# Four graph layers on one core: the first two mask units of layers 0 and 1 are made during the dense product, and the last group of layer 3 is multiplied tile by tile

## What is computed

```python
# layer 0 (4 heads of 64; layer 1 is the same form with slope 0.2 and no elu)
h = einsum('nf,hfd->hnd', x, W)
s_src = einsum('hnd,hd->hn', h, a[:, :64, 0]); s_dst = einsum('hnd,hd->hn', h, a[:, 64:, 0])
e = leaky_relu(s_src[:, :, None] + s_dst[:, None, :], 0.01)
alpha = softmax(where(adj == 0, -inf, e), axis=-1)
out = elu(einsum('hij,hjd->hid', alpha, h))
# layer 2: one wide head with a gated side branch (matrix work only, unchanged here)
# layer 3
t = tanh(x @ W + b); e = (t @ a)[:, 0]; valid = sum(t, axis=1) != 0
w = where((adj > 0) & valid, exp(e - max), 0)
out = (w / sum(w)) @ (x @ W)
```

## Time and profile before

| | us |
|---|---|
| median of 3 runs | 3078.27 |
| lowest and highest of them | 3075.31, 3078.79 |
| the profiled execution, by the same clock | 3075.53 |
| its span in the trace | 3073.7 |
| PE busy in it | 2958.1 (96%) |
| DVE, ACT, POOL busy | 2141.2, 1921.2, 1171.3 |
| mean granted clock of PE | 0.989 |

### The profile page before, as it was taken

One profiled execution on the slowest core, in us unless ns is written; L12 is line 12 of the kernel. 1 busy time (PEld: TensorE's weight loads), 2 busy tenths in 40 slices (PEclk: granted clock), 3 DMA queues, 4 the chain that ended last, 5 costly groups with the idle time before them and its releaser, 6 DMA issues.

```text
span 3073.7 us, 65208 instructions
## 1 busy us (share of the span) xinstructions
PE 2958.1 (96%) x24628; PEld 2584.4 (84%) x24628; DVE 2141.2 (70%) x3861; ACT 1921.2 (63%) x3414; POOL 1171.3 (38%) x1555
## 2 busy tenths in 40 slices
PE   7899999999979999999999999999999999889998
PEld 6799999999969999999997877887778778655554
DVE  4998888888879888888886556665666565562245
ACT  4777898999979999999995544454455444430000
POOL 0571375642225656564221023333323332534222
PEclk9999999999999999999999999999999999989999
DMA  8566200000100000000010000000000000000001
GB/s 285 184 215 234 70 14 11 14 11 15 60 12 12 14 11 14 11 14 11 14 34 12 4 1 4 4 1 4 1 4 4 1 1 1 2 1 0 1 21 35
DMA packets 41977, 104.55 MB, mean 34 GB/s; under 512 B 9921, under 2 KB 23489, under 8 KB 33601
## 3 DMA queue, kind: packets, MB, share of 16 engines
q1 hardware_dynamic: 39584, 101.61, 10.0%
q10 hardware_dynamic: 2208, 0.52, 0.1%
HBM read 97.73 MB, written 4.39 MB: 33 GB/s over the span
## 4 chain that ended last, share of the span: by engine, by line
PE 77%; DVE 2%; ACT 2%; issue 1%; POOL 1%; POOLq 0%; DVEq 0%; ACTq 0%
PE bank L1318 16%; PE bank L1315 16%; PE bank L1372 15%; PE bank L1410 12%; PE bank L1321 11%; PE bank L1399 2%; PE bank L1256 2%; PE bank L1386 1%; ACT above L932 0%; PE bank L1527 0%; DVE rings L1931 0%; ACT rings L1072 0%; DVE rings L1936 0%; ACT values L845 0%; PE bank L1494 0%
## 5 line engine op out<-in xcount | busy, mean ns | idle before, releaser
L1315 PE MATMUL bank<-values,rings 128*128 128x195 bf16 x8192 | 1415.9, 247 | 43.4 <-DVE rings L1936 39.7
L1318 PE MATMUL bank<-values,rings 128*128 128x195 bf16 x8192 | 1416.1, 249 | 0.0
L932 ACT ACTIVATE above<-srow,kpass 128x512 fp8e4<-128x512 f32 x2048 | 1290.2, 709 | 124.2 <-DVE rings L1936 118.0
L1315 PEld LDWEIGHTS bank<-values,rings 128*128 128x128 fp8e4 x8192 | 806.9, 98 | 53.2 <-issue 51.0
L1318 PEld LDWEIGHTS bank<-values,rings 128*128 128x128 fp8e4 x8192 | 789.5, 96 | 0.7
L1931 DVE TENSOR_TENSOR rings<-rings,above 128x512 uint32<-128x512 uint32 x512 | 399.2, 780 | 186.5 <-PE bank L1318 165.4
L1025 ACT ACTIVATE values<-srow,cmul 128x512 f32<-128x512 f32 x256 | 205.8, 814 | 428.0 <-PE bank L1410 427.2
L1936 DVE TENSOR_TENSOR rings<-rings 128x512 uint32<-128x512 uint32 x512 | 431.2, 842 | 17.2
L1410 PE MATMUL bank<-hv,values 128*128 128x257 f32 x1792 | 420.6, 380 | 0.0
L1410 PEld LDWEIGHTS bank<-hv,values 128*128 128x128 f32 x1792 | 335.0, 190 | 69.9 <-issue 25.2
L1321 PE MATMUL bank<-values,rings 128*128 128x390 bf16 x2032 | 338.6, 329 | 13.4 <-DVE values L1730 13.4
(11 more groups left out here) (217 smaller groups left out, 3445.0 us busy)
## 6 DMA issues: line engine op xcount, KB each, us to landing
arena<-in_adj_dram SPq DMA_DIRECT2D x64, 1024.0 KB, 5.1
srow<-src_dram SPq DMA_DIRECT2D x69, 256.0 KB, 3.1
x<-in_x_dram SPq DMA_DIRECT2D x4, 1024.0 KB, 12.5
out_dram<-x SPq DMA_DIRECT2D x7, 512.0 KB, 2.9
arena<-in_L_gnn_fe_w_dram SPq DMA_DIRECT2D x2, 512.0 KB, 6.2
arena<-in_L_gnn_W_hz_dram SPq DMA_DIRECT2D x1, 1024.0 KB, 7.3
arena<-in_L_gnn_g_w_dram SPq DMA_DIRECT2D x1, 1024.0 KB, 10.8
weights<-in_L_gnn_W_dram SPq DMA_DIRECT2D x3, 256.0 KB, 3.8
```

The source lines that it names most:

```text
L932: last = act.activation(above[:, k % 2, q, :], srow[:, par, :], ACT.Relu, scale=BIG, bias=kpass[:, p % 2, k * Q + q:k * Q + q + 1], satura ...
L1315: pe.matmul(acc[:, 0:KW], pos[:, k % 2, q, :].bitcast(FP8)[:, rows], v[:, 0:KW], start=start, stop=final, skip_group_check=True)
L1318: last = pe.matmul(acc[:, KW:2 * KW], neg[:, k % 2, q, :].bitcast(FP8)[:, rows], v[:, KW:2 * KW], start=False, stop=final, skip_group_chec ...
```

## The change

1. **Masks ahead.** In layers 0 and 1 PE spreads the first row after quad 3 (`first_row`, into bank 7) instead of after the last quad. ACT copies it in quad 4 and writes two of the eight `above` pieces of units 0 and 1 in each of the quads 4 to 7 (`above_ahead`), from column scores of the first eight tiles that DVE scales early (`first_keys`). DVE makes the masks of both units before `stats` (`masks_ahead`). At the start of attention the values of round 0 stand alone.
2. **Row factors later.** POOL's `row_factors` waits for the first two values, and ACT takes their exponential at the end of its group 0.
3. **Weights of layer 0.** The loads of `a` are two transfers instead of eight, and `fold_first_weights` does four instructions twice as wide instead of eight.
4. **Layer 2 to 3.** POOL adds the bias of the pairs 10 to 13. In layer 3's unit 1, `first_lasts` of round 0 goes ahead of `first_products` of round 1.
5. **Last group.** During group 6 DVE makes a second copy of masks, those of group 7 (eight instructions, into the arena). PE then does group 7 one bank after the other, 32 matmuls each (`last_tiles`). DVE takes out group 6 and normalises the quads 5 and 6 after group 6's units, and normalises each tile of the last quad at once; SP stores each by itself.

The diff, cut to its core:

```diff
+UNITS_AHEAD = 2
+ROW_AT, KEYS_AT = 3, 2
+BY_POOL = range(10, 14)
...
-            for t in range(T - QT, T, 2):
-                sp.wait_ge(s_xmade, T * NORMS[4] + t + 2)
-                sp.dma_start(out[t * P:(t + 2) * P, :].rearrange("(t p) f -> p t f", p=P), x[:, t:t + 2, :])\
-                    .then_inc(s_out, 16)
+            for t in range(T - QT, T):
+                sp.wait_ge(s_xmade, T * NORMS[4] + t + 1)
+                sp.dma_start(out[t * P:(t + 1) * P, :], x[:, t, :]).then_inc(s_out, 16)
...
+        edge_last = arena[:, 0:BITS * Q * WORDS].bitcast(U32).rearrange("p (k q w) -> p k q w", k=BITS, q=Q)
...
             def row_factors(l):
-                pool.wait_ge(s_shift, l + 1)
+                pool.wait_ge(s_vfirst, first_values_before(l) + 2)
...
+                for n in BY_POOL:
+                    pool.wait_ge(E.l_h, n + 1)
+                    pool.wait_ge(E.l_score, n - 1)
+                    pool.tensor_tensor(low3[n % 2], h[:, n * ET:(n + 1) * ET, :],
+                                       bvec[:, :].unsqueeze(1).to_broadcast([P, ET, F]), ALU.add).then_inc(E.l_inpool, 1)
...
+            def copy_row(l):
+                act.wait_ge(s_rowps, l + 1)
+                act.activation(srow[:, 0, :], bank[7][:, :], ACT.Copy).then_inc(s_srow[0], 16)
+
+            def above_ahead(l, n):
+                k, q = divmod(2 * n, Q)
+                if n == 0:
+                    act.wait_ge(s_kfirst, l + 1)
+                    act.wait_ge(s_srow[0], (l * H * NG // 2 + 1) * 16)
+                if q == 0:
+                    act.wait_ge(s_sides, l * H * UNITS + k - 1 + CREDIT)
+                for q in (q, q + 1):
+                    last = act.activation(above[:, k % 2, q, :], srow[:, 0, :], ACT.Relu, scale=BIG,
+                                          bias=kpass[:, 0, k * Q + q:k * Q + q + 1], saturate=False)
+                if q == Q - 1:
+                    last.then_inc(s_above, 1)
...
-                for hd in range(H):
-                    act.dma_start(avec[:, s, hd * D:(hd + 1) * D],
-                                  A["L0_gnn_a"][hd, s * D:(s + 1) * D, 0].partition_broadcast(P)).then_inc(s_w, 16)
+                act.dma_start(avec[:, s, :].rearrange("p (h d) -> p h d", h=H),
+                              A["L0_gnn_a"][:, s * D:(s + 1) * D, 0].partition_broadcast(P)).then_inc(s_w, 16)
...
                         copy_quad_xT(l, q)
+                        if l < 2 and q == ROW_AT + 1:
+                            copy_row(l)
+                        if l < 2 and q > ROW_AT:
+                            above_ahead(l, q - ROW_AT - 1)
                         copy_quad_h(l, q)
...
+            def first_row(l):
+                pe.wait_ge(s_h, T * l + GT + 1)
+                if l == 0:
+                    pe.wait_ge(s_packed, ROW_AT - 1 + CREDIT)
+                for it in range(GT):
+                    last = pe.transpose(bank[7][:, it * P:(it + 1) * P],
+                                        scores[:, 0, it:it + 1].to_broadcast([P, P]), ident[:, :])
+                last.then_inc(s_rowps, 1)
...
+            def last_tiles(slot, par):
+                for it in range(GT):
+                    rows = slice(it * P, (it + 1) * P)
+                    for j in range(T):
+                        if it == 0 and j % Q == 0:
+                            pe.wait_ge(s_lastedge, j // Q + 1)
+                        last = pe.matmul(bank[GT * par + it][:, 0:2 * KW],
+                                         edge_last[:, j // Q, j % Q, :].bitcast(FP8)[:, rows], values[:, slot, j, :],
+                                         start=(j == 0), stop=(j == T - 1))
+                    last.then_inc(s_bank, 1)
...
+            def masks_ahead(l):
+                chain.enter(0, LINKS[l])
+                if l == 0:
+                    dve.wait_ge(s_packed, GT + CREDIT)
+                for k in range(UNITS_AHEAD):
+                    for _ in masks(l, TURN[l] * H * UNITS + k, k, packed[:, :, 0:WORDS]):
+                        pass
...
-                      1: ((first_products, 1), (first_lasts, 0), (first_rests, 1), (first_products, 2), (first_lasts, 1)),
+                      1: ((first_lasts, 0), (first_products, 1), (first_rests, 1), (first_products, 2), (first_lasts, 1)),
...
-                with dve.Fori(1, NG // 2) as gg:
+                with dve.Fori(1, NG // 2 - 1) as gg:
                     for par in range(2):
                         group(3, gg * 2 + (last_pass + par), gg, par, 1 - par, norm=gg * 2 + (par - 2))
+                group(3, last_pass + NG - 2, NG // 2 - 1, 0, 1, norm=NG - 4, last_edges=True)
+                evacuate(3, 0, 0, last_pass + NG - 1)
+                chain.enter(NG - 3, 2)
+                for k in (2, 3, 4, 6, 7):
+                    output_norm(QUADS - 3, k)
                 chain.leave(NG - 2)
-                for k in (2, 3, 4):
+                for k in (2, 3, 4, 6, 7):
                     output_norm(QUADS - 2, k)
                 last_rows()
```

147 lines of the change are left out of this document (86 added, 61 removed).

## The result

The changed kernel takes 3058.54 us in the median of four runs (3057.64 to 3061.66), the kernel before 3077.03 in the runs beside them: a ratio of 0.9946, 95% interval 0.9935 to 0.9958. Faster by 0.54%, or 18.5 us by these medians. Three later groups of runs of the kernel before had medians of 3076.41, 3076.13 and 3076.16, and four more runs of the changed kernel had 3059.67, so the gain is 16.5 to 18.5 us. The prediction was 3060.5, range 3054 to 3067.

What follows compares the result with a forecast made beforehand. PE was taken as the bound, busy 2958.1 of 3073.7 us. Terms 1.4 - 0.5 + 5.7 + 5.5 + 0.9 + 1.3 + 2.3 = 16.6 us gave 3058.9 (profiled base) or 3061.7 (median); predicted 3060.5, range 3054 to 3067.

Steps and rivals of the forecast that it cites:

- Start of layer 0: Wait for folded weights before PE's first product: two loads 0.3 us and wide fold 1.1 us, 1.4 earlier; bounds 0.5 and 4.
- rival of a still earlier start: Layer 0: both loads of a land with the first of eight, dense product up to 5 us earlier; total 3057.5, chance 0.08.
- The row in the dense product: Layers 0 and 1: four spreading transposes move between quads, where PE is waited for, costing 0.5 us in each layer.
- Layer 0, first group: Start of layer 0's attention: PE starts 4.2 us earlier, later units 5.8; term 5.7, bounds 4.2 and 6.5.
- given back later: Layer 0, groups 1 to 3: DVE sets the pace, both first groups' 11.2 us are lost; total 3070.1, chance 0.10.
- Layer 1, first group: Start of layer 1's attention: unit 2 begins 6.0 us earlier, less 0.5 for the row; term 5.5, bounds 3.6 and 7.
- Between layers 2 and 3: Four bias adds moved from DVE to POOL: 3.8 us per two pairs against 4.2, gain 0.9; bounds -0.5 and 2.4.
- POOL and DVE slow each other: Lower bound for moving four bias adds to POOL between layers 2 and 3: -0.5 us instead of a gain.
- fear of the program change: Reduction before layer 3 follows POOL's last add and needs a change of POOL's program: may take 0.4 us, at most 1.
- Start of layer 3: Last parts of round 0 move ahead of round 1's products: gain 1.3 us, bounds 0.5 and 1.5.
- The end: PE's end to DVE's last normalisation: 8.2 us instead of 10.5, gain 2.3; bounds 0 and 5.
- Masks late: Layers 0 and 1: unit 1's `above` delays DVE's masks, `stats` slips up to 3.6 us each; total 3067.5, chance 0.05.

## Why the prediction was right, and where it was not

The sum was 16.6 us and the gain is 16.5 to 18.5. The mechanism came true in its largest part, the masks ahead, and the total also by luck, as the terms show:

- **Start of layer 0**: 1.4 predicted, 2.5 to 2.8 measured. The fold's 1.1 was right. The step that failed is "Two loads carry the same bytes, so I take 0.3 us for them": it was 1.45. The bound of 4 held it. The rival of a still earlier start had the mechanism but asked for 5. In the kernel without masks ahead only 1.65 of the 2.5 reach the end of group 0, and 1.35 the pass near 498, so the 1.4 is near what the start is worth by luck.
- **The row in the dense product**: 0.5 predicted, 0.43 measured in layer 1, from its first dense product to the statistics (40.71 before, 41.14 in all eight profiles with the row). In layer 0 the clock's differences, of up to 1 us there, hide it.
- **Layer 0, first group**: PE's start 4.2 earlier against the statistics, predicted and measured (10.70 to 6.48). The further 1.5, from DVE's shorter list, came in whole in four profiles (39.44 against 40.91) and by 0.4 or less in the other four (40.76), with the place of the clock's lower stretches. At group 0 the sum has 1.4 - 0.5 + 5.7 = 6.6; the eight profiles have 5.9 to 8.4. Of this lead 0.15 to 0.65 us went again by group 8 in six of them, one gained 0.6, and one lost 2.6, 1.5 of it at a lower stretch near 267. With what the early start loses, "given back later" has that much truth.
- **Layer 1, first group**: 5.5 predicted, 4.8 to 5.4 measured.
- **Between layers 2 and 3**: +0.9 predicted, -0.15 to -0.6 measured. The step that failed is the sum "Tanh 0.9, score 1.4, add 1.3 and signals make 3.8 us", made of durations taken where the other engine was quiet; the waits for the tanh grew instead, from 1.0 to 2.4. "POOL and DVE slow each other" stood only as a bound, of -0.5. The fear of the program change (0.4 us) was not borne out, if narrowly.
- **Start of layer 3**: 1.3 predicted, 1.0 measured, and 1.2 to 1.35 in the three profiles of the new order without the longer idle time left open above.
- **The end**: from PE's end to the last normalisation 8.2 predicted and 8.2 measured; before 10.5. Inside it POOL's root for quad 5 came 0.7 us later than counted, and each of the four tiles took 3.47 instead of 3.6, which cancels most of it. With the smaller last store 2.75 instead of 2.3.
- **Masks late**: the chance of 0.05 was for a case that the first profile showed for 0.9 us and the others not. The cover of 6.46 was counted as if the conversions kept their place. In fact they wait longer for the adjacency after an earlier start: DVE's waits for these loads were 26 us and are 31 to 39 in the eleven other profiles. In the three with an earlier start and no masks ahead, DVE's idle time before the statistics is 3.1, 4.0 and 4.3 instead of 6.46. With the 3.6 of masks in it, 0 to 1.3 are left in the eight profiles.

The misses at their own places (start +1.2, adds -1.3, layer 1 -0.4, layer 3 -0.3, end +0.4) nearly cancel, so the total is better than its parts. The profile's own difference of 13.8 would have pointed at a lost 3 us that no instruction explains. 1.5 of it lies near 498 and goes with the clock there, as the twelve profiles together show; the differences of two profiles alone could not have told.

## What to carry over

A step that runs in an idle stretch of an engine uses up the cover of all others there: after moving work, count the stretch again, with the loads as they now fall. Price work moved between DVE and POOL by rows in which both are busy; single durations make it look better than it is. And before explaining a difference of 1 to 3 us at one place between two profiles, look at the granted clock behind PE's waits there, in more than one execution. A gain at the start of a layer is worth only what is left of it some groups later; read the lead there too.

## Of the hardware, not expected

- A wait of PE of 2.9 us was followed by 6 us at a granted clock of 0.50, 0.72 or 1.00 in three executions of the same instructions. The spread between undisturbed runs of one kernel, 2 to 6 us, is of the size of a few such places.
- Matmuls that compute nothing, put into PE's waits ahead of the attention of layers 1 and 3, left a clock of 1.00 in the six microseconds behind them (two profiles), where the ten profiles without them have 0.52 to 0.73. With those near 498 they saved 3.4 us by the medians.
- Eight small loads landed 1.45 us later than two that carried the same bytes (one profile each; 1.2 to 1.7 over all twelve).
- Beside POOL's 128x512 adds (1.1 to 1.3 us each), one of DVE's products on 128x512 took 1.55 us instead of 0.69, in all seven profiles, and others 0.68 to 0.80.
